# Conditioned residual stack (three adapter layers and paged attention): the first sequence's low parts moved from VectorE to GpSimd

## The chip, the cores and the metric

The kernel runs on 1 core of one Trainium2 chip. The metric is the time of one execution on the device in microseconds. Before the change it is 2490.15 us, the median of 3 runs (2487.76 to 2490.87).

## The reference

The input `x` is 64 sequences of 32 tokens with 512 features, float32. Four layers are added to it, one after the other:

```
x = x + x @ W0[adapter]^T                                 # per-sequence weight, 8 adapters
x = x + x @ W1^T + bias + scale * (x @ A1^T) @ B1^T       # LoRA of rank 16, 8 adapters
x = x + x @ W2^T + b + 2 * (x @ A2) @ B2                  # LoRA of rank 16, 32 slots
x = x + attention(x)
```

The attention projects to 32 query heads, 8 key heads and 8 value heads of 128. Queries and keys are divided by their root mean square, scaled and rotated by position. Each sequence attends to 512 cached keys, which a block table finds in 64 pages of 32 (masked beyond the sequence's length), and to its own 32 keys. Four query heads share one key head. Then comes the softmax, the product with the values and an output projection:

```
k_all = concat([k_cache[block_table], k], axis=1)
scores = where(valid, einsum('bqhd,bkhd->bhqk', q, k_all) / sqrt(128), -1e30)
o = einsum('bhqk,bkhd->bqhd', softmax(scores), v_all)
return einsum('bse,de->bsd', o, Wo)
```

## The kernel before

The kernel runs in stages on one core: `layer0` (to about 115 us), `lora_layers` (to about 290), `qkv` (the projections, to about 915), `attention` (to about 2390 with the start of the last stage inside it) and `output_projection`. Data between stages goes through DRAM.

Products whose precision matters are made in three passes (`three_pass`, lines 108 to 110). Each float32 operand is split into a high part, rounded by ScalarE to the matmul's own format (`fp32r`), and a low part, which is the operand minus its high part. The three products are high by high, high by low and low by high. The low parts are subtractions of two SBUF or PSUM operands.

**The projections.** `qkv` works through chunk pairs `b` of 32 steps `j`: 16 tiles of 128 tokens for each of two chunks of 512 columns (4 heads). The pair 0 makes the values, pairs 1 to 4 the queries, pair 5, the last, the keys. In every step after the values, TensorE multiplies tile `j` (12 matmuls of 512 columns) and turns the result of 4 steps before with four transposes (line 879). ScalarE takes the root of the sum of squares of the step before (`rms`, line 696), scales that step's product (`normed`, line 705, four instructions), squares the new product (line 690) and copies the turned tile of 4 steps before to `out_t` (line 715), which SyncE stores (line 640). VectorE's order in a step is: the first half of `part_b` of step j-2 (line 824), the reciprocal of step j-1 (`inv_rms`, line 808), `part_a` of step j-2 (line 817), the second half of `part_b` (line 824), their sum `rotated` (line 834), and the sum of squares of step j (line 812). `normed`, the tables `same` and `cross`, `part_a`, `part_b` and `rotated` all lie in SBUF. `normed` waits for the reciprocal, the reciprocal for the root, and the root for the sum of squares. In the steps 3, 6, 9 and 12 of a chunk a quarter of the next chunk's weights is split as well (lines 592 and 608). TensorE waits before a multiplication for the `normed` of four steps before (`normed_ready`), since the PSUM buffers turn round, and before a transpose for `rotated` and for the `out_t` copy of two steps before.

**What attention does ahead, in the last pair.** The first sequence's keys and queries are prepared while the last pair runs. There are six pieces: four of the cached keys (4 pages each, 128x1024), one of queries (128x1024, piece 3) and the sequence's own keys (128x256, piece 5). SyncE loads the pages in the steps of `PAGES_AHEAD`, GpSimd loads queries (`load_q`, line 1154) and own keys (`load_own_k`, line 1160). ScalarE makes the high part of a piece in the steps 13, 15, 17, 19, 21 and 25, at the end of its step (`scalar_ahead`, `hi_part`, line 1041, counted by `hi_done`). VectorE makes the low part one step later, at the end of its step (`vector_ahead`, `lo_part`, line 1051, counted by `lo_done`):

```
PIECES_AHEAD = {13: 0, 15: 1, 17: 2, 19: 3, 21: 4, 25: 5}
        if j - 1 in PIECES_AHEAD:
            lo_part(dve, 0, 0, PIECES_AHEAD[j - 1])
```

TensorE makes the scores of head 0 behind the last multiplication (step 31) and those of head 1 in the step behind that. Before head 0 it waits for all six low parts (`lo_done`). From then on the engines go over to attention. VectorE makes the low parts of all other sequences there, two steps of heads after the first scores at the earliest, and SyncE's page loads for later sequences wait for `lo_done` too.

**GpSimd's queue.** After the tables of the rotation (lines 673, 675 and 680, at 352 to 377 us) GpSimd has no work until the last pair. Its program in `attention` then is: wait for the stores of all queries, `load_q(0, 0)`; wait for the store of the keys of the first tile and for the row list; `load_own_k(0, 0)`; wait for the values' stores and the end of all projections (`mm_done`); a memset of the mask's columns, the loads of the second sequence's queries and own keys, a memset, and the value gathers of the first sequence.

**Attention.** For each of the 64 sequences and 8 key heads TensorE makes scores, transposes of the probabilities (line 1343) and the product with the values (line 1366). ScalarE makes the exponentials (line 1056), VectorE the mask and maximum (line 1080), and GpSimd the value gathers and the stores of the output.

Of the kernel before, what the change touches and what calls it, by code (L numbers as in the profile page):

```python
# [21 lines left out]
ALU = mybir.AluOpType  # L22
# [21 lines left out]
def f32(ap):  # L44

    return ap.bitcast(fp32)
# [66 lines left out]
def later(t, n):  # L113

    return not isinstance(t, int) or t >= n


def in_pairs(eng, n, body):

    body(0, False)  # L120
    with eng.Fori(1, n - 1) as i:
        body(i, False)
    body(n - 1, True)
# [354 lines left out]
ALL_STEPS = STEPS * (NB - 1)  # L478
# [455 lines left out]
PIECES_AHEAD = {13: 0, 15: 1, 17: 2, 19: 3, 21: 4, 25: 5}  # L934
# [15 lines left out]
def attention(nc, m, place, both, output, pool_sems, k_pages, v_pages, table, lens, key_at, q_t, k_own, v_own, o_t, inv_t):  # L950
# [34 lines left out]
    hi_done, lo_done, s_done, masked, pv_done = m.sem("hi_done"), both.lo_done, both.s_done, both.masked, both.pv_done  # L985
# [5 lines left out]
    def piece(c, p):  # L991

        if c == PIECE_Q:
            return q_raw[p][:, :], *(b[p][:, :, :].rearrange("p h q -> p (h q)") for b in (q_hi, q_lo))
        at, n = pages_of(c)
        return (k_raw[p][:, at:at + n, :].rearrange("p n (h k) -> p n h k", h=HK),
                *(b[p][:, :, at * PSIZE:(at + n) * PSIZE].rearrange("p h (n k) -> p n h k", n=n) for b in (k_hi, k_lo)))
# [33 lines left out]
    def raw_read(s, c):  # L1031

        return PIECES if not later(s, 3) else PIECES * (s - 2) + PIECE_TURN[c]
# [6 lines left out]
            act.wait_ge(s_done, HK * (s - 1))  # L1040
        act.activation(hi, raw, ACT.Copy).then_inc(hi_done, 1)  # L1041

    def lo_part(dve, s, p, c):

        raw, hi, lo = piece(c, p)
        turn = TURN_AHEAD[c] if not later(s, 1) else PIECES * s + PIECE_TURN[c]
        dve.wait_ge(hi_done, turn)
        if c == PIECE_Q and later(s, 1) and not later(s, 2):
            for n in range(2):
                dve.wait_ge(both.stored[n], 16 * ALL_STEPS // 2)  # L1050
        dve.tensor_tensor(lo, raw, f32(hi), ALU.subtract).then_inc(lo_done, 1)  # L1051

    def exponential(act, u, j):
        b = j % NB_P
# [16 lines left out]
    def make_mask(dve, s, p):  # L1071

        dve.tensor_scalar(mask[:, p, 0:NKEY], key_sb[:, :], lens_f[:, bass.ds(s, 1)], MASKED,
                          ALU.is_ge, ALU.mult).then_inc(lens_and_masks, 1)
        dve.wait_ge(lens_and_masks, s + 2)

    def mask_and_max(dve, u, j):

        b = j % NB_P
        dve.tensor_tensor_reduce(  # L1080
            out=prob[:, b, :].rearrange("p (a n) -> p a n", a=2), in0=ps_s[:, j % 2, :, 0:HALF],
            in1=mask[:, j // HK, :].rearrange("p (a n) -> p a n", a=2), scale=-SM_SCALE, scalar=3e38, op0=ALU.add, op1=ALU.min,
            accum_out=shift[:, b:b + 1]).then_inc(masked, 1)

    def vector_ahead(dve, j):

        if j == 4:
            dve.wait_ge(small_loaded, 48)
            dve.tensor_copy(lens_f[:, :], lens_sb[:, :]).then_inc(lens_and_masks, 1)
        if 4 <= j < 4 + PPP:  # L1090
            at = slice((j - 4) * PSIZE, (j - 3) * PSIZE)
            dve.tensor_copy(row_f[at, :], table_sb[at, :].rearrange("p (n m) -> p n m", m=PPP)[:, :, j - 4])\
               .then_inc(rows_ready, 1)
        if j == 4 + PPP:
            dve.wait_ge(rows_ready, PPP)
            dve.tensor_scalar(row_f, row_f, float(PSIZE), step_sb[:, 0:1], ALU.mult, ALU.add).then_inc(rows_ready, 1)
        if j == 5 + PPP:
            dve.wait_ge(rows_ready, PPP + 1)
            dve.tensor_copy(row_sb[:, :], row_f).then_inc(rows_ready, 1)
        if j - 1 in PIECES_AHEAD:  # L1100
            lo_part(dve, 0, 0, PIECES_AHEAD[j - 1])
        if j == STEPS:
            dve.wait_ge(lens_and_masks, 1)
            dve.wait_ge(zeroed, 2)
            make_mask(dve, 0, 0)
            dve.wait_ge(s_done, 1)
            mask_and_max(dve, 0, 0)
# [42 lines left out]
    def gpsimd(pool):  # L1150
        def load_q(s, p):
            if later(s, 2):
                pool.wait_ge(lo_done, raw_read(s, PIECE_Q))
            pool.dma_start(q_raw[p][:, :], q_t[bass.ds(s, 1)].rearrange("s d g x -> s d (g x)"))\
                .then_inc(k_loaded[p][PIECE_Q], 16)

        def load_own_k(s, p):
            if later(s, 2):
                pool.wait_ge(lo_done, raw_read(s, PIECE_OWN))
            pool.dma_start(k_raw[p][:, NPP, :], k_own[bass.ds(s, 1)]).then_inc(k_loaded[p][PIECE_OWN], 16)  # L1160

        def gather(s, p, c):

            pool.indirect_dma_start(  # L1164
                v_sb[p][:, c, :], None, v_pages.rearrange("n k x -> (n k) x"),
                bass.IndirectOffsetOnAxis(ap=rows_now[:, p, c:c + 1], axis=0)).then_inc(v_loaded[p], 16)

        def load_values(s, p):

            rows = v_own[bass.ds(s * SEQ, SEQ), :].rearrange("k (g u d) -> k g u d", g=HK // OG, u=OG)  # L1170
            for u in range(OG):
                if later(s, 2) and not u:
                    pool.wait_ge(pv_done, HK * (s - 1))
                if u == 1:
                    pool.tensor_copy(rows_now[:, p, :], row_sb[:, bass.ds(s * (NPP // PPP), NPP // PPP)])\
                        .then_inc(rows_copied, 1)
                    pool.wait_ge(rows_copied, s + 1)
                pool.dma_start(vo_sb[p][u * SEQ:(u + 1) * SEQ, :, u, :], rows[:, :, u, :])\  # L1178
                    .then_inc(own_v_loaded[p], 16)
                if u:  # L1180
                    gather(s, p, u - 1)

        def store_o(s, p):
            pool.wait_ge(o_ready, (HK // OG) * (s + 1))
            pool.dma_start(o_t[bass.ds(s, 1)], o_sb[:, p, :, :].rearrange("p h q -> p (h q)"))\
                .then_inc(o_stored[p], 16)

        def store_inv(s, p):
            pool.wait_ge(inv_ready, s + 1)
            pool.dma_start(inv_t[bass.ds(s, 1)].rearrange("s (h q) -> (s h) q", h=HK), inv_sb[:, p, :])\  # L1190
                .then_inc(inv_stored[p], 16)

        for p in range(2):
            pool.wait_ge(both.stored[p], 16 * (STEPS // 2) * (NB - 2))
        load_q(0, 0)
        pool.wait_ge(both.stored[0], 16 * ((STEPS // 2) * (NB - 2) + NT // 2 + 1))
        pool.wait_ge(rows_ready, PPP + 2)
        load_own_k(0, 0)
        for p in range(2):
            pool.wait_ge(both.v_stored[p], 16 * STEPS // 2)  # L1200
        pool.wait_ge(both.mm_done, ALL_STEPS)
        pool.memset(mask[:, :, NKEY:NALL], 0.0).then_inc(zeroed, 1)
        load_q(1, 1)
        load_own_k(1, 1)
        pool.memset(vo_sb[0][:, :, :, :], 0.0).then_inc(zeroed, 1)
        pool.wait_ge(zeroed, 3)
        load_values(0, 0)
        gather(0, 0, OG - 1)
        for p in range(2):
            pool.wait_ge(both.stored[p], 16 * ALL_STEPS // 2)  # L1210
        pool.memset(vo_sb[1][:, :, :, :], 0.0).then_inc(zeroed, 1)
        pool.wait_ge(zeroed, 4)

        def pair(i, last):


            for p in range(2):
                s = 2 * i + p
                if not last:
                    load_q(s + 2, p)  # L1220
                    load_own_k(s + 2, p)
                if not (last and p):
                    load_values(s + 1, 1 - p)
                if later(s, 1):
                    store_o(s - 1, 1 - p)
                if not (last and p):
                    gather(s + 1, 1 - p, OG - 1)
                if later(s, 1):
                    store_inv(s - 1, 1 - p)

        in_pairs(pool, NSEQ // 2, pair)
        store_o(NSEQ - 1, 1)
        store_inv(NSEQ - 1, 1)
# [102 lines left out]
    def tensor(pe):  # L1336
# [51 lines left out]
        in_pairs(pe, NSEQ // 2, pair)  # L1388

    return Ahead(sync_ahead, scalar_ahead, vector_ahead, tensor_ahead), Programs(sync, gpsimd, scalar, vector, tensor)  # L1390


# [727 lines left out]
```

## Time and profile before

| | before |
|---|---|
| median of 3 runs | 2490.15 us (2487.76 to 2490.87) |
| the profiled execution, its own time | 2487.61 us |
| its span | 2486.1 us |
| mean granted TensorE clock | 0.991 |
| TensorE matmul busy | 2414.1 us (97%) |
| VectorE busy | 1798.8 us (72%) |
| ScalarE busy | 1589.1 us (64%) |
| GpSimd busy | 696.5 us (28%) |
| HBM | 217 GB/s over the span |

All times of rows are microseconds from the start of the span of this one execution. Engines in the rows: PE is TensorE, PEld its weight load, DVE VectorE, ACT ScalarE, POOL GpSimd, SP SyncE. L12 is line 12 of the kernel. An instruction's recorded duration holds about 0.1 us of overlap with the next one on VectorE and ScalarE, so starts are compared with starts. The granted clock is a share of 2.4 GHz; 0.50 is the lower level, 1.2 GHz.

### The profile page before, as it was taken

How to read it: one execution, taken by the hardware profiler on the slowest of the kernel's cores; microseconds unless marked ns; L12 is line 12 of the kernel's file. 1: busy time of each engine (PE TensorE's matmuls, PEld its weight loads, DVE VectorE, ACT ScalarE, POOL GpSimd, SP SyncE). 2: the span in 40 equal slices, each digit the busy share in tenths (PEclk: the TensorE clock that was granted, in tenths of full speed). 3: DMA queues.
4: the chain of work that ended last, by engine and by line, in shares of the span. 5: the costliest groups of instructions: out<-in, count | busy, mean ns of one | idle time of the engine just before them, and what ended most of it. 6: DMA issues, size and time to landing. Idle time of an engine off the chain costs nothing.

```text
span 2486.1 us, 55755 instructions
## 1 busy us (share of the span) xinstructions
PE 2414.1 (97%) x16326; PEld 2196.7 (88%) x16327; DVE 1798.8 (72%) x3705; ACT 1589.1 (64%) x3325; POOL 696.5 (28%) x930
## 2 busy tenths in 40 slices
PE   6699999999999989999999999999999999999999
PEld 4588788888888779999999999999999999788887
DVE  6345445989998988888888887888888888644443
ACT  3122236777777778888888888888888888311111
POOL 1222130000000025455455445545445544000000
PEclk9899999999999999999999999999999999999999
DMA  7422442333333479888888888888888887766663
GB/s 240 140 76 76 147 140 89 101 102 112 102 98 102 128 211 313 294 290 295 304 285 293 302 290 287 289 305 285 297 300 283 295 300 269 271 228 213 211 210 138
DMA packets 377285, 541.48 MB, mean 218 GB/s; under 512 B 49522, under 2 KB 263218, under 8 KB 374386
## 3 DMA queue, kind: packets, MB, share of 16 engines
q1 hardware_dynamic: 305074, 316.33, 39.7%
q0 software_dynamic: 70016, 221.30, 25.8%
q10 hardware_dynamic: 2112, 2.89, 0.4%
q8 instruction: 34, 0.56, 0.1%
q14 instruction: 49, 0.40, 0.1%
HBM read 442.06 MB, written 98.30 MB: 217 GB/s over the span
## 4 chain that ended last, share of the span: by engine, by line
PE 62%; DMA 1%; DVE 1%; ACT 0%; issue 0%; DVEq 0%
PE both_ps_o L1366 18%; PE both_ps_s L108 10%; PE both_ps_s L110 10%; PE both_ps_s L109 10%; PE both_ps_pt L1343 9%; PE both_ps_o L1369 5%; DMA out_w<-in_wo 1%; PE both_ps_s L1349 1%; PE both_ps_s L1351 0%; DVE out_w_lo L1461 0%; ACT att_prob L1056 0%; DVE out_o_lo L1479 0%; DVE out_o L1475 0%; ACT out_w_hi L1457 0%; DVE att_prob L1080 0%
## 5 line engine op out<-in xcount | busy, mean ns | idle before, releaser
L1366 PE MATMUL both_ps_o<-att_pt,att_v 128*128 128x128 f32 x4096 | 539.3, 275 | 0.0
L1056 ACT ACTIVATE att_prob<-att_prob,att_shift 128x544 f32<-128x544 f32 x512 | 384.0, 750 | 204.7 <-DVE att_shift L1080 194.9
L1366 PEld LDWEIGHTS both_ps_o<-att_pt,att_v 128*128 128x128 f32 x4096 | 504.0, 191 | 0.0
L1080 DVE CUSTOM_DVE_ANT_0 att_prob<-both_ps_s,att_mask 128x544 f32<-128x544 f32 x512 | 365.9, 715 | 0.0
L1051 DVE TENSOR_TENSOR att_k_lo<-att_k_raw,att_k_hi 128x1024 fp32r<-128x1024 f32 (+1 forms) x320 | 338.2, 1057 | 1.9 <-ACT att_k_hi L1041 1.9
L108 PE MATMUL both_ps_s<-att_k_hi,att_q_hi 128*128 128x272 f32 x1024 | 338.3, 330 | 0.7 <-issue 0.6
L1164 POOL DMA_INDIRECT att_v<-in_v_pages,att_rows_now x256 | 299.6, 1170 | 85.0 <-issue 83.8
L1343 PE MATMUL both_ps_pt<-both_ident,att_prob 128*128 128x128 f32 x2048 | 308.2, 273 | 0.9 <-ACT att_pt L1240 0.9
L110 PE MATMUL both_ps_s<-att_k_hi,att_q_lo 128*128 128x272 f32 x1024 | 297.2, 290 | 0.0
L1240 ACT ACTIVATE att_pt<-both_ps_pt 128x512 f32<-128x512 f32 x512 | 294.8, 576 | 0.1
L109 PE MATMUL both_ps_s<-att_k_lo,att_q_hi 128*128 128x272 f32 x1024 | 294.4, 288 | 0.0
L1041 ACT ACTIVATE att_k_hi<-att_k_raw 128x1024 fp32r<-128x1024 f32 (+1 forms) x320 | 292.8, 915 | 0.0
L1178 POOL DMA_DIRECT2D att_vo<-v_own x256 | 144.4, 564 | 501.7 <-PE both_ps_o L1369 451.0
L1274 DVE COPY att_p_own<-att_prob 128x32 f32<-128x32 f32 x512 | 96.6, 189 | 221.9 <-PE both_ps_s L110 174.8
L1343 PEld LDWEIGHTS both_ps_pt<-both_ident,att_prob 128*128 128x128 f32 x2048 | 242.0, 142 | 1.3 <-ACT att_prob L1056 0.9
L1468 ACT ACTIVATE out_o_hi<-out_o 128x2048 fp32r<-128x2048 f32 x32 | 61.4, 1919 | 264.9 <-DVE out_o L1475 264.9
L108 PE MATMUL both_ps_s<-out_w_hi,out_o_hi 128*128 128x512 f32 x512 | 201.6, 394 | 5.5 <-DVE out_o_lo L1479 3.5
L110 PE MATMUL both_ps_s<-out_w_hi,out_o_lo 128*128 128x512 f32 x512 | 201.2, 393 | 0.0
L109 PE MATMUL both_ps_s<-out_w_lo,out_o_hi 128*128 128x512 f32 x512 | 201.2, 393 | 0.0
L1369 PE MATMUL both_ps_o<-att_pto,att_vo 128*128 128x128 f32 x1024 | 198.2, 275 | 0.0
L108 PEld LDWEIGHTS both_ps_s<-att_k_hi,att_q_hi 128*128 128x128 f32 x1024 | 194.3, 190 | 2.6 <-issue 1.1
L109 PEld LDWEIGHTS both_ps_s<-att_k_lo,att_q_hi 128*128 128x128 f32 x1024 | 195.2, 191 | 0.0
(195 smaller groups left out, 5153.1 us busy)
## 6 DMA issues: line engine op xcount, KB each, us to landing
att_k_raw<-in_k_pages SPq DMA_DIRECT2D x1024, 128.0 KB
q_t<-qkv_out_t SPq DMA_DIRECT2D x128, 256.0 KB, 2.3
att_q_raw<-q_t POOLq DMA_DIRECT2D x64, 512.0 KB
o_t<-att_o POOLq DMA_DIRECT2D x64, 512.0 KB, 6.7
out_o<-o_t SPq DMA_DIRECT2D x32, 1024.0 KB, 6.9
out_inv<-inv_t SPq DMA_DIRECT2D x32, 1024.0 KB, 6.9
qkv_w_stage<-in_w_qkv SPq DMA_DIRECT2D x12, 1024.0 KB, 5.2
early_stage<-in_w SPq DMA_DIRECT2D x10, 1024.0 KB, 7.0
```

Of the source, the lines that this page charges most:

```text
L108: pe.matmul(out, xh, wh, start=start, stop=False)
L109: pe.matmul(out, xh, wl, start=False, stop=False)
L110: return pe.matmul(out, xl, wh, start=False, stop=stop)
L1041: act.activation(hi, raw, ACT.Copy).then_inc(hi_done, 1)
L1051: dve.tensor_tensor(lo, raw, f32(hi), ALU.subtract).then_inc(lo_done, 1)
L1056: act.activation(prob[:, b, :], prob[:, b, :], ACT.Exp, bias=shift[:, b:b + 1], scale=-1.0, accum_out=total[:, j // HK, j % HK:j % HK + 1] ...
L1080: dve.tensor_tensor_reduce(out=prob[:, b, :].rearrange("p (a n) -> p a n", a=2), in0=ps_s[:, j % 2, :, 0:HALF], in1=mask[:, j // HK, :].re ...
L1164: pool.indirect_dma_start(v_sb[p][:, c, :], None, v_pages.rearrange("n k x -> (n k) x"), bass.IndirectOffsetOnAxis(ap=rows_now[:, p, c:c + ...
L1240: act.activation(pt_sb[:, j % OG, :, :], ps_pt[:, j % 2, :, :], ACT.Copy).then_inc(pt_ready, 1)
L1343: mm = pe.transpose(ps_pt[:, j % 2, c, :], prob[:, j % NB_P, c * P:(c + 1) * P], ident[:, :])
L1366: pe.matmul(out, v_sb[p][:, c, h * DH:(h + 1) * DH], pt_sb[:, j % OG, c, :], start=(c == 0), stop=False)
L1369: pe.matmul(out, vo_sb[p][:, g % 2, j % OG, :], pto_sb[:, g % 2, :], start=False, stop=True).then_inc(pv_done, 1)
```

## The change

`lo_part` is given the engine, and the six low parts of the first sequence are no longer issued in VectorE's last projection steps but in GpSimd's program. The first four (pieces 0, 1, 2, 3) stand behind `load_q(0, 0)`, each behind its wait for ScalarE's high part; the last two (pieces 4, 5) behind `load_own_k(0, 0)`. The instruction is the same subtraction and counts the same semaphore. All other sequences' low parts stay on VectorE.

```
-    def lo_part(dve, s, p, c):
+    def lo_part(eng, s, p, c):
 
         raw, hi, lo = piece(c, p)
         turn = TURN_AHEAD[c] if not later(s, 1) else PIECES * s + PIECE_TURN[c]
-        dve.wait_ge(hi_done, turn)
+        eng.wait_ge(hi_done, turn)
         if c == PIECE_Q and later(s, 1) and not later(s, 2):
             for n in range(2):
-                dve.wait_ge(both.stored[n], 16 * ALL_STEPS // 2)
-        dve.tensor_tensor(lo, raw, f32(hi), ALU.subtract).then_inc(lo_done, 1)
+                eng.wait_ge(both.stored[n], 16 * ALL_STEPS // 2)
+        eng.tensor_tensor(lo, raw, f32(hi), ALU.subtract).then_inc(lo_done, 1)
...
-        if j - 1 in PIECES_AHEAD:
-            lo_part(dve, 0, 0, PIECES_AHEAD[j - 1])
         if j == STEPS:
...
         load_q(0, 0)
+        first_pieces = list(PIECES_AHEAD.values())
+        for c in first_pieces[:4]:
+            lo_part(pool, 0, 0, c)
         pool.wait_ge(both.stored[0], 16 * ((STEPS // 2) * (NB - 2) + NT // 2 + 1))
         pool.wait_ge(rows_ready, PPP + 2)
         load_own_k(0, 0)
+        for c in first_pieces[4:]:
+            lo_part(pool, 0, 0, c)
         for p in range(2):
             pool.wait_ge(both.v_stored[p], 16 * STEPS // 2)
         pool.wait_ge(both.mm_done, ALL_STEPS)
```

## Rows read from the trace of the kernel before

**Rows 1.** What TensorE waited for, 846 to 915 us: us in total, times, longest.

```profile
PE both_ps_o L879 <- ACT qkv_out_t L715: 6.3, 7, 2.3
```

**Rows 2.** Chain that ended last, in order of time: start us, us, what.

```profile
912.78 0.70 DVE qkv_rotated L834
```

**Rows 3.** VectorE's groups, 846 to 903 us: count, busy us, mean ns, idle before.

```profile
L1051 DVE TENSOR_TENSOR att_k_lo<-att_k_raw,att_k_hi 128x1024 fp32r<-128x1024 f32 x4 | 4.9, 1214 | 0.0
```

**Rows 4.** ScalarE's timeline, one high part: start us, us, instruction, idle before.

```profile
861.68 1.09 ACT L1041 ACTIVATE att_k_hi<-att_k_raw 128x1024 fp32r<-128x1024 f32 x1
```

**Rows 5.** VectorE's timeline, one pair of steps with a piece.

```profile
862.99 0.18 DVE L808 RECIPROCAL qkv_inv_rms<-qkv_rms 128x4 f32<-128x4 f32 x1 [0.60 <-ACT qkv_rms L696]
863.09 0.66 DVE L817 TENSOR_TENSOR qkv_part_a<-qkv_normed,qkv_same 128x512 f32<-128x512 f32 x1
...
864.87 0.69 DVE L812 TENSOR_REDUCE qkv_sumsq<-qkv_squares 128x4 f32<-128x512 f32 x1
...
866.94 0.17 DVE L808 RECIPROCAL qkv_inv_rms<-qkv_rms 128x4 f32<-128x4 f32 x1
...
870.42 0.18 DVE L808 RECIPROCAL qkv_inv_rms<-qkv_rms 128x4 f32<-128x4 f32 x1 [0.60 <-ACT qkv_rms L696]
```

**Rows 6.** VectorE's timeline, plain steps and the step with the small low part.

```profile
887.66 0.18 DVE L808 RECIPROCAL qkv_inv_rms<-qkv_rms 128x4 f32<-128x4 f32 x1
...
890.59 0.18 DVE L808 RECIPROCAL qkv_inv_rms<-qkv_rms 128x4 f32<-128x4 f32 x1
...
893.07 0.42 DVE L1051 TENSOR_TENSOR att_k_lo<-att_k_raw,att_k_hi 128x256 fp32r<-128x256 f32 x1
...
893.74 0.17 DVE L808 RECIPROCAL qkv_inv_rms<-qkv_rms 128x4 f32<-128x4 f32 x1
```

**Rows 7.** GpSimd's table products and VectorE's weight subtractions, timeline, 354 to 379 us.

```profile
354.03 2.40 POOL L675 TENSOR_TENSOR qkv_cross<-qkv_sincos,qkv_norm 128x1024 f32<-128x1024 f32 x1
354.19 2.78 DVE L608 TENSOR_TENSOR qkv_w_lo<-qkv_w_stage,qkv_w_hi 128x512 fp32r<-128x512 f32 x1 [13.45 <-ACT qkv_w_hi L592]
...
361.56 2.40 POOL L673 TENSOR_TENSOR qkv_same<-qkv_sincos,qkv_norm 128x1024 f32<-128x1024 f32 x1
362.35 2.15 DVE L608 TENSOR_TENSOR qkv_w_lo<-qkv_w_stage,qkv_w_hi 128x512 fp32r<-128x512 f32 x1 [5.38 <-ACT qkv_w_hi L592]
...
378.67 0.69 DVE L608 TENSOR_TENSOR qkv_w_lo<-qkv_w_stage,qkv_w_hi 128x512 fp32r<-128x512 f32 x1 [6.62 <-ACT qkv_w_hi L592]
```

**Rows 8.** GpSimd's bias sums and a VectorE instruction beside them, timeline, 119 to 142 us.

```profile
119.81 3.61 POOL L1769 TENSOR_TENSOR lora_xb<-lora_x,early_stage 128x512 f32<-128x512 f32 x1 [2.54 <-DMA lora_x<-x]
...
131.17 2.51 POOL L1769 TENSOR_TENSOR lora_xb<-lora_x,early_stage 128x512 f32<-128x512 f32 x2 [7.75 <-DVE lora_x L1858]
131.39 0.69 DVE L1824 TENSOR_TENSOR lora_xt_lo<-both_ps_s,lora_xt_hi 128x512 fp32r<-128x512 f32 x1 [0.38 <-ACT lora_xt_hi L1786]
...
140.34 1.29 POOL L1769 TENSOR_TENSOR lora_xb<-lora_x,early_stage 128x512 f32<-128x512 f32 x1 [6.66 <-DVE lora_x L1858]
```

**Rows 9.** ScalarE's sines, GpSimd's start behind them and its slowest instructions, timeline.

```profile
349.50 2.01 ACT L736 ACTIVATE qkv_sincos<-qkv_wrapped 128x1024 f32<-128x1024 f32 x2
...
351.65 2.41 POOL L673 TENSOR_TENSOR qkv_same<-qkv_sincos,qkv_norm 128x1024 f32<-128x1024 f32 x1 [66.95 <-ACT qkv_sincos L736]
...
371.59 5.85 POOL L680 TENSOR_SCALAR qkv_cross<-qkv_cross 128x1024 f32<-128x1024 f32 x2
```

**Rows 10.** GpSimd's load of own keys, and TensorE's last turning transposes, timelines.

```profile
876.18 0.56 POOL L1160 DMA_DIRECT2D att_k_raw<-k_own  x1 [60.71 <-DMA k_own<-qkv_out_t]
...
900.26 0.60 PE L879 MATMUL both_ps_o<-both_ident,qkv_rotated 128*128 128x128 f32 x4
...
903.45 0.60 PE L879 MATMUL both_ps_o<-both_ident,qkv_rotated 128*128 128x128 f32 x4
```

**Rows 11.** TensorE behind a gap; then 1 us by engine (PE, PEld, DVE, ACT, POOL), clock, DMA.

```profile
43.02 0.66 PE L418 MATMUL l_ps_t<-l_ident,l_x 128*128 128x128 f32 x4 [1.64 <-DMA l_x<-in_x]
...
909.00:910.00 1.00, 0.00 (x0) 0.00 (x0) 0.91 (x3) 0.74 (x3) 1.00 (x1) 0.67 1.17 348
```

## The prediction

> **What bounds the kernel now.** I read the busy shares, then TensorE's waits, then the timelines of the last projection steps, and last the chain of waits over the hand-over to attention. TensorE is busy for 97% of the span, so VectorE time is worth something only where TensorE waits for it. Between 846 and 915 us it does: 6.3 us of waits at the turning transposes (line 879), for ScalarE's `out_t` copies [rows 1]. The chain enters attention through the last `rotated` [rows 2]. Between 858 and 915 us the pace is thus set by a loop of VectorE and ScalarE, and TensorE only follows. After it attention is paced by TensorE, so a shift of this hand-over reaches the end of the kernel whole.
>
> The loop per step: reciprocal (VectorE), `normed` and squares (ScalarE), sum of squares (VectorE), root (ScalarE), next reciprocal. A plain step takes 2.93 us from reciprocal to reciprocal [rows 6]. TensorE needs 3.19 us a step, as its turning transposes at 900.26 and 903.45 show [rows 10], so there the loop only catches up what it is behind. A pair of steps with one piece of the first sequence takes 7.43 us [rows 5]: 3.95 for the step that holds the low part, 3.48 for the one that holds the high part. TensorE's pair would be 6.4.
>
> **What the change removes.** Six low parts leave VectorE: five of 1024 columns at 1.21 us [rows 3] and one of 256 at 0.42 [rows 6]. A large one costs the loop 3.95 - 2.93 = 1.02 us. The small one costs 3.15 - 2.93 = 0.22. Removed from the loop: 5 x 1.02 + 0.22 = 5.32 us. With them gone a pair would take 6.41 us, as long as TensorE's, so most of the waits inside the projections would go too. If nothing came back, the hand-over would be 5.3 us earlier.
>
> **What it adds.** Six subtractions on GpSimd, each with two SBUF inputs. The nearest rows are GpSimd's 128x1024 products of lines 673 and 675 at 2.40 us [rows 7]. GpSimd is idle here, so its own time is free; its neighbours' is not. In the same rows two weight subtractions of VectorE, two SBUF inputs, normally 0.69 us, started while a GpSimd product ran and took 2.78 and 2.15. Taking off the usual length, they really began at 356.29 and 363.82 us, each 2.26 after the start of the GpSimd product. So such a product holds VectorE off for its whole length less 0.14. A VectorE instruction that reads one input from PSUM is not held: 0.69 us beside GpSimd [rows 8]. And when VectorE is already in a row of two-input instructions, GpSimd can be the one that waits: the first of its 128x512 sums took 3.61 us instead of 1.29 [rows 8].
>
> The Trainium skill says the same as a rule (SBUF — State Buffer, "SBUF: two separate sides"): the port pair shared by VectorE and GpSimd is an exclusive lock for a whole instruction, and a VectorE instruction with two SBUF inputs competes for it with a GpSimd one that reads SBUF. By this rule the change swaps a short occupation of VectorE for a longer blockade; the trace agrees, with 2.78 us against 0.69.
>
> Which VectorE instructions meet it? `part_a`, both halves of `part_b` and `rotated` have two SBUF inputs. The order in the loop decides. ScalarE's high part is followed by its root, and the reciprocal and `part_a` come right behind. Take the pair at 862 us: high part 861.68 + 1.09 = 862.77 [rows 4]. GpSimd starts 0.14 after a ScalarE result (349.50 + 2.01 = 351.51 to 351.65 [rows 9]), so at 862.91. `part_a` would start at 863.09 [rows 5], 0.18 later, and finds the port taken until 862.91 + 2.26 = 865.17: delayed by 2.08. From `part_a` on VectorE has no slack, since it reaches its sum of squares (1.88 us after the reciprocal) as soon as ScalarE has the squares; the next reciprocal is 2.08 later. Against 1.02 removed that is **+1.06 per large piece**, 5.3 for five. The small one: a line through 1.29 (512 columns) and 2.40 (1024) gives 0.74, 0.60 of it holding; GpSimd starts at 890.44 and holds until 891.04, `part_a` is due at 890.68 (a reciprocal at 890.59 [rows 6] and 0.09), so 0.36 against 0.22 removed, +0.14. **Sum +5.4 us.**
>
> Bounds of the unknown form (GpSimd writing the rounded low part over key strides): below, GpSimd comes too late for `part_a`, waits out VectorE's row of two-input instructions and starts with the sum of squares; then only what sticks out over that sum's 0.69 us [rows 5] delays, 2.26 - 0.69 = 1.57, +0.55 a piece, nothing for the small one (-0.22), +2.5 in all. Lowest of all, no blockade: -5.3. Above, each takes 2.93 us, half of the 5.85 of two, GpSimd's slowest instructions of this size [rows 9], +0.53 a piece, +8.1 in all. I take 2.40, the row with two inputs and the same size.
>
> **What moves with it.** TensorE is throttled by the loop from 858 us on, so its last projection, the page loads that wait for it, SyncE's stores, the mask memset and the value gathers all shift with the hand-over; SyncE's queue has no new wait. On GpSimd's queue the load of the first sequence's own keys is now behind the fourth low part. It is issued at 876.18 after waiting for a store [rows 10]; its high part, one pair behind the one at 861.68, ends at 870.2, and with 2.4 us the low part at 872.6, so the load keeps its time. The last low part then ends near 891 plus the shift of some 5 us, and the scores of the first head, which wait for all six, come behind the transposes at 903.45 [rows 10], with the same shift: 12 us of cover, so I cost this wait at nothing. Without the cover its price would be whatever the last piece is late. The memsets and gathers behind it wait for the end of the projections and are not passed. The high parts stay on ScalarE at their places. The executions before give 2487.61 for the profiled one (span 2486.1); with 5.4 that is 2493.0. The median of the runs, 2490.15, is 2.5 above it, so I predict **2495.6 us**. What a measurement of this kernel can tell from no change is 0.2%, 5.0 us; the forecast is just past it.
>
> **Rivals.**
> *No blockade.* GpSimd's subtraction runs beside `part_a` for free, 1.02 a piece comes back: 2490.15 - 5.3 = 2484.8, faster. For it: nothing but that the fp32r form is untried and that a fresh start may take the port later than 0.18 us after it is shown. Against it: both subtractions of [rows 7] were held. Chance 0.12, of which 0.08 past 0.2%.
> *GpSimd comes second.* VectorE's row of two-input instructions keeps the port, as in [rows 8]; +2.5, so 2492.7. The margin is 0.18 us, and it decides at zero. Chance 0.17, same.
> *TensorE's clock falls.* It now idles some 2.1 us per pair instead of 1.0. In the trace 1.64 us idle is followed by four transposes in 0.66 us, full clock, and at 909 us, after gaps of 1.5 and 2.3, the granted clock is down to 0.67 [rows 11]. At 1.2 GHz, the lower level, a step takes some 6 us against the loop's 4.2, so three steps at it lose 5 us more: 2500.8, slower. A gap of 2 us at one place in each pair decides. Chance 0.06.
> *First scores wait for GpSimd.* Needs a low part of over 12 us; in the 0.65 below.
>
> **How the numbers follow.** The forecast has 0.65. With the spread of the runs (2487.76 to 2490.87) and the uncertain length, three fifths of it are past 5.0 us: 0.39 slower, 0.26 same. With the rivals: slower 0.39 + 0.06 and 0.02 from longer instructions among the second rival's; same 0.26 + 0.15 + 0.04; faster 0.08. The range leaves out the first rival and part of the third: down to the second in a low run, 2487.76 + 2.5 = 2490.3, taken as 2490, up to the long bound in a high run, 2490.87 + 8.1 = 2499.
>
> **What would show it.** Right: `part_a` (line 817) of 2.7 us instead of 0.66 in five steps, reciprocals 5.0 and 3.5 us apart, more waits of TensorE at line 879, the last reciprocal 5 us later. Wrong: `part_a` at 0.66 throughout and a pair of 6.4 us (no blockade); GpSimd subtractions of 4 us and a late `part_b` (second rival); a granted clock under 1 between 858 and 900 us (third).

## The result and the profile after

The changed kernel takes 2495.47 us in the median of 17 runs (2490.22 to 2499.38), the kernel before 2490.15 in the median of 17 (2486.55 to 2493.44). The ratio is 1.002 with a 95% interval of 1.0013 to 1.0026: slower, by 5.0 us (3.2 to 6.5). Whether it is past the 5.0 us that the prediction set as its threshold stays open.

| | before | after |
|---|---|---|
| the profiled execution, its own time | 2487.61 us | 2497.33 us |
| its span | 2486.1 us | 2495.8 us |
| mean granted TensorE clock | 0.991 | 0.991 |
| VectorE busy | 1798.8 us | 1804.4 us |
| GpSimd busy | 696.5 us | 712.0 us |
| TensorE matmul busy | 2414.1 us | 2414.2 us |

VectorE lost six instructions and is 5.6 us busier. Where that comes from is seen in the timelines of the last projection steps. Here is the second piece after the change, out of the timelines of VectorE, ScalarE and GpSimd. [rows 4, 5] show the third piece before; the five large pieces are alike. The columns are start us, us, instruction, idle time before it; "..." stands for further lines of the timeline.

```profile
858.79 1.10 ACT L1041 ACTIVATE att_k_hi<-att_k_raw 128x1024 fp32r<-128x1024 f32 x1
...
859.96 2.40 POOL L1051 TENSOR_TENSOR att_k_lo<-att_k_raw,att_k_hi 128x1024 fp32r<-128x1024 f32 x1 [5.98 <-ACT att_k_hi L1041]
860.10 0.18 DVE L808 RECIPROCAL qkv_inv_rms<-qkv_rms 128x4 f32<-128x4 f32 x1 [0.60 <-ACT qkv_rms L696]
860.19 2.71 DVE L817 TENSOR_TENSOR qkv_part_a<-qkv_normed,qkv_same 128x512 f32<-128x512 f32 x1
...
863.94 0.68 DVE L812 TENSOR_REDUCE qkv_sumsq<-qkv_squares 128x4 f32<-128x512 f32 x1
...
864.98 0.18 DVE L808 RECIPROCAL qkv_inv_rms<-qkv_rms 128x4 f32<-128x4 f32 x1
```

GpSimd starts 0.07 us behind the end of the high part (858.79 + 1.10 = 859.89). `part_a` is issued 0.23 later and lasts 2.71 instead of 0.66: it really began at 862.24, 2.28 after GpSimd. The step that follows, with the next high part, still takes 3.49 us from reciprocal to reciprocal (to 868.47), the one in which GpSimd subtracts 4.88 instead of 3.95. The pair takes 8.37 instead of 7.43. All five large pieces look like this (`part_a` 2.72, 2.71, 2.72, 2.72 and 2.72 us). The small one takes GpSimd 0.78 us from 898.69 on, and `part_a` beside it 1.02.

TensorE's waits for `rotated` between 846 and 924 us (in total, times, longest):

```profile
PE both_ps_o L879 <- DVE qkv_rotated L834: 7.1, 5, 1.6
```

All five lie in the steps with pieces (855 to 890 us). Before, TensorE waited there four times for `out_t`, 0.55 us each, 2.2 us in total. The rest of the 6.3 us in [rows 1], 4.1 us, lies behind 904 us, at the hand-over to attention; so [rows 1] says less about the steps with pieces than the prediction took from it. After the change the `out_t` waits at the hand-over come to 6.2 us. TensorE's idle time rose in the steps with pieces, but its clock stayed at full speed. One window of the changed kernel, columns: length, busy of PE, PEld, DVE, ACT and POOL with counts, granted clock, DMA share, GB/s:

```profile
858.00:880.00 22.00, 17.99 (x85) 13.39 (x84) 19.79 (x30) 15.50 (x40) 7.20 (x3) 1.00 0.22 60
```

From 880 to 900 us the granted clock is 1.00 as well.

The span differs by 9.7 us, more than the runs do. The reciprocals split it (a reciprocal is named by the step in which VectorE issues it). In step 3, before the change touches anything, the profiled execution after is 3.3 us later (812.60 against 809.28); that is the scatter of the stages before. From there to step 14 it loses 0.3, over the 18 steps from the reciprocal of step 14 to the last one 4.74 (65.00 against 60.26 us), over the hand-over, up to TensorE's first transpose of attention's own probabilities (924.48 us before, 933.40 after), 0.6, and 0.8 in the 1560 us behind. The 4.74 are the change; whether the 0.6 belong to it is taken up behind the rivals.

From here on this stretch of 18 steps serves as the measure of the loop. Each kernel's was profiled once, but in all eight profiles the steps that no subtraction touches last 2.91 to 2.94 us, or 3.48 to 3.50 with a high part, while whole executions scatter by several us.

### The profile page after: what moved, and what is told of

It reads as the page before. It is cut to its first block, busy times and chain, and to the rows that moved or that the text cites. A ratio compares the mean times of both kernels' runs of the same rounds, so it can differ in the third digit from the quotient of the medians.

```text
span 2495.8 us, 55755 instructions
## 1 busy us (share of the span) xinstructions
PE 2414.2 (97%) x16326; PEld 2196.3 (88%) x16327; DVE 1804.4 (72%) x3699; ACT 1587.9 (64%) x3325; POOL 712.0 (29%) x936
## 4 chain that ended last, share of the span: by engine, by line
PE 61%; DMA 1%; ACT 1%; DVE 1%; issue 0%; ACTq 0%; DVEq 0%
PE both_ps_o L1369 18%; PE both_ps_s L108 10%; PE both_ps_s L110 10%; PE both_ps_s L109 9%; PE both_ps_pt L1346 9%; PE both_ps_o L1372 5%; DMA out_w<-in_wo 1%; PE both_ps_s L1352 1%; PE both_ps_s L1354 0%; DMA k_own<-qkv_out_t 0%; ACT att_prob L1056 0%; ACT att_k_hi L1041 0%; DVE out_w_lo L1464 0%; DVE out_o_lo L1482 0%; DVE out_o L1478 0%
## 5 line engine op out<-in xcount | busy, mean ns | idle before, releaser
L1051 DVE TENSOR_TENSOR att_k_lo<-att_k_raw,att_k_hi 128x1024 fp32r<-128x1024 f32 x315 | 333.2, 1058 | 1.9 <-ACT att_k_hi L1041 1.9
L1162 POOL DMA_INDIRECT att_v<-in_v_pages,att_rows_now x256 | 305.0, 1191 | 85.0 <-issue 83.8
```

Of the source, the lines that this page charges most:

```text
L1051: eng.tensor_tensor(lo, raw, f32(hi), ALU.subtract).then_inc(lo_done, 1)
L1162: pool.indirect_dma_start(v_sb[p][:, c, :], None, v_pages.rearrange("n k x -> (n k) x"), bass.IndirectOffsetOnAxis(ap=rows_now[:, p, c:c + ...
```

## The experiments

The theory was: GpSimd's subtractions hold VectorE's two-input instructions for their length, this sets the loop back, and the loop's shift reaches the end whole. Four kernels tested its parts against the rivals; two more asked whether GpSimd can be used without the hold.

**A fill instead of the subtraction.** GpSimd writes zeros. Its queue, waits and order stay; the low parts of the first sequence are left out of the computation.

```
+        if not later(s, 1):
+            eng.memset(f32(lo), 0.0).then_inc(lo_done, 1)
+            return
         eng.tensor_tensor(lo, raw, f32(hi), ALU.subtract).then_inc(lo_done, 1)
```

> GpSimd fills the first sequence's six low parts with zeros instead of subtracting (they are left out of the computation; waits, order and semaphores as in the changed kernel). Theory (a blockade by GpSimd instructions that read SBUF, and its shift reaches the end whole): part_a 0.66 us in every step, reciprocals 2.93 and 3.48 us apart in a pair, the last reciprocal 5 us earlier than in the kernel before, time 5.3 us under it (ratio 0.998). Rival A (any GpSimd instruction holds VectorE): a fill of 1.0 us delays part_a by some 0.65 us, pair 7.1 us, ratio 0.9993. Rival B (the changed kernel is slower for GpSimd's queue or the later own-key load, not for the blockade): the time stays at that of the changed kernel, ratio 1.002.

Measured: 2484.96 us against 2489.93 before, ratio 0.9979 (0.9970 to 0.9988). Timelines of GpSimd and VectorE:

```profile
863.10 0.95 POOL L1052 MEMSET att_k_lo<- 128x1024 f32 x1 [5.45 <-ACT att_k_hi L1041]
863.26 0.18 DVE L808 RECIPROCAL qkv_inv_rms<-qkv_rms 128x4 f32<-128x4 f32 x1 [0.60 <-ACT qkv_rms L696]
863.36 0.66 DVE L817 TENSOR_TENSOR qkv_part_a<-qkv_normed,qkv_same 128x512 f32<-128x512 f32 x1
...
869.67 0.18 DVE L808 RECIPROCAL qkv_inv_rms<-qkv_rms 128x4 f32<-128x4 f32 x1 [0.60 <-ACT qkv_rms L696]
```

`part_a` starts 0.26 us into a 0.95 us fill and takes its usual 0.66. The pair takes 6.41 us, the 18 steps 54.89, 5.37 less than before. Both rivals fall: an instruction that only writes does not hold VectorE, and the order in GpSimd's queue, with the load of the own keys behind four pieces, costs nothing. It also gives the price of six low parts on VectorE, 5.4 us of loop, and shows that this arrives at the end.

**A copy instead of the subtraction**, with one SBUF input; the subtraction of the first sequence's high parts is left out.

```
+        if not later(s, 1):
+            eng.tensor_copy(lo, raw).then_inc(lo_done, 1)
+            return
         eng.tensor_tensor(lo, raw, f32(hi), ALU.subtract).then_inc(lo_done, 1)
```

> GpSimd copies the raw piece into the low part (one SBUF input instead of two; the low parts of the first sequence are wrong values, the subtraction is left out). Theory (every GpSimd instruction that reads SBUF takes the shared port for its length): part_a in the five steps grows by the copy's duration less 0.14 less the 0.2 us of its head start; if the copy takes 1.2 us, part_a is 1.5 us. Rival (only two-input GpSimd instructions hold): part_a stays 0.66 us and the pair takes 6.4 us.

```profile
862.26 1.04 POOL L1052 CAST att_k_lo<-att_k_raw 128x1024 fp32r<-128x1024 f32 x1 [5.96 <-ACT att_k_hi L1041]
...
862.51 1.33 DVE L817 TENSOR_TENSOR qkv_part_a<-qkv_normed,qkv_same 128x512 f32<-128x512 f32 x1
```

`part_a` is held for 0.67 us: it began at 863.18, 0.92 after GpSimd. The copy takes 1.04, so it too holds for its length less 0.12, as the theory had it. Reading one operand is enough. The step costs the loop 0.59 us (3.52 against 2.93), the 18 steps take 57.89. One execution, 2486.27 us, too few to compare the time.

**The subtraction moved behind the squares**, so that it meets the sum of squares first; `j` is the step of the piece's high part.

```
+        def late(c):
+            j = [j for j, piece_at in PIECES_AHEAD.items() if piece_at == c][0]
+            pool.wait_ge(both.squared, STEPS * (NB - 2) + j + 2)
+            lo_part(pool, 0, 0, c)
+
         for c in first_pieces[:4]:
-            lo_part(pool, 0, 0, c)
+            late(c)
...
```

> Each GpSimd subtraction waits also for ScalarE's squares of the next step, so that it starts with VectorE's sum of squares instead of with part_a. Theory (the hold counts only where VectorE has a two-input instruction due; the sum of squares has one input and runs beside it): part_a back to 0.66 us, the first half of part_b delayed by 1.6 to 1.7 us, next reciprocal 1.6 us late instead of 2.0, time 2.5 us over the kernel before (ratio 1.001). Rival (VectorE is held whatever its instruction reads): the sum of squares itself takes 2.7 us and the time is that of the changed kernel, ratio 1.002.

```profile
866.93 0.69 DVE L812 TENSOR_REDUCE qkv_sumsq<-qkv_squares 128x4 f32<-128x512 f32 x1
866.98 2.38 POOL L1051 TENSOR_TENSOR att_k_lo<-att_k_raw,att_k_hi 128x1024 fp32r<-128x1024 f32 x1 [5.61 <-ACT qkv_squares L690]
867.53 2.10 DVE L824 TENSOR_TENSOR qkv_part_b<-qkv_normed,qkv_cross 128x256 f32<-128x256 f32 x1
```

The sum of squares (one input) takes its 0.69 us beside GpSimd. The first half of `part_b` behind it is held 1.68 us, and the step takes 4.51 to 4.54. The 18 steps take 62.91 us, 2.65 over before, 2.09 under the change. Time: 2491.67 against 2489.93, ratio 1.0006 (0.9997 to 1.0015), so not shown to be slower than before by the time alone, and its interval just overlaps the changed kernel's (1.0013 to 1.0026). The difference between these kernels rests on the loop. The same subtraction on the same engine costs the loop 1.6 us instead of 2.0 when it starts some 2 us later in the step.

**VectorE, but in its idle time**: the kernel before, with four low parts at the head of the steps 16, 18, 20 and 22.

```
+LO_FIRST = {16: 0, 18: 1, 20: 2, 22: 3}
...
+                if is_last(b) and j in LO_FIRST:
+                    ahead.vector_first(dve, j)
                 if is_step(b, j, 2):
                     cross_part(*step_before(b, j, 2), 0)
...
-        if j - 1 in PIECES_AHEAD:
+        if j - 1 in PIECES_AHEAD and PIECES_AHEAD[j - 1] not in LO_FIRST.values():
             lo_part(dve, 0, 0, PIECES_AHEAD[j - 1])
...
+    def vector_first(dve, j):
+        lo_part(dve, 0, 0, LO_FIRST[j])
```

> The kernel before, with the low parts of pieces 0 to 3 still on VectorE but at the head of the steps 16, 18, 20 and 22, where VectorE sits idle 0.6 to 0.7 us for ScalarE's root behind the next high part. Theory (the loop is what counts, and idle VectorE time inside it is free): each such low part costs the loop 0.45 instead of 1.02 us, together 2.2 us, ratio 0.9991. Rival (VectorE's total work sets the pace, not its place): no change against the kernel before, ratio 1.000.

```profile
862.70 0.18 DVE L808 RECIPROCAL qkv_inv_rms<-qkv_rms 128x4 f32<-128x4 f32 x1
...
865.18 1.21 DVE L1053 TENSOR_TENSOR att_k_lo<-att_k_raw,att_k_hi 128x1024 fp32r<-128x1024 f32 x1
...
866.65 0.17 DVE L808 RECIPROCAL qkv_inv_rms<-qkv_rms 128x4 f32<-128x4 f32 x1
...
869.57 0.18 DVE L808 RECIPROCAL qkv_inv_rms<-qkv_rms 128x4 f32<-128x4 f32 x1
```

The steps take 3.95 and 2.92 instead of 3.95 and 3.48: a low part now shares a step with the next piece's high part, and the 0.60 us for which VectorE waited are filled. The 18 steps take 57.90 us (-2.36), so the place in the loop counts and not VectorE's total work. Ratio 0.9991 (0.9982 to 1.0000), 2488.38 us against 2489.93; the size is the expected one, and the interval just reaches no change, so by the time alone the gain is not shown.

**Small slices at the right moment.** Pieces 0, 1, 2 and 4 on GpSimd in four slices of 256 columns, one per step, each released by that step's squares; piece 3 in VectorE's idle time of step 22; the small piece on VectorE as before.

```
+        for n in range(16):
+            pool.wait_ge(both.squared, STEPS * (NB - 2) + 14 + n + 1)
+            lo_slice(pool, LO_POOL[n // 4], n % 4)
+            if n == 8:
+                pool.wait_ge(both.stored[0], 16 * ((STEPS // 2) * (NB - 2) + NT // 2 + 1))
+                pool.wait_ge(rows_ready, PPP + 2)
+                load_own_k(0, 0)
```

> The low parts of pieces 0, 1, 2 and 4 on GpSimd in four slices of 256 columns each, one slice per step 14 to 29, each started by ScalarE's squares of that step, so that it runs beside VectorE's sum of squares (one input, 0.6 us); piece 3 on VectorE in the idle time of step 22, the own keys on VectorE as in the kernel before; the load of own keys behind the ninth slice. Theory (a hold costs only what sticks out over one-input VectorE time): a slice holds the port 0.60 to 0.64 us from 0.14 us behind the squares, sticks out 0.15, costs the loop 0 to 0.1 a step. The 18 steps from the first high part to the last reciprocal take 54.9 + 0.5 + 0.2 + (0 to 1.6) = 55.6 to 57.2 us against 60.3 in the kernel before; ratio 0.9981 to 0.9988. Rival (every crossing of a GpSimd subtraction costs VectorE its whole length wherever it is put): 16 x 0.64 = 10 us on top of 55.6, slower than the kernel before, ratio 1.002.

```profile
856.40 0.69 DVE L812 TENSOR_REDUCE qkv_sumsq<-qkv_squares 128x4 f32<-128x512 f32 x1
856.45 0.74 POOL L1071 TENSOR_TENSOR att_k_lo<-att_k_raw,att_k_hi 128x256 fp32r<-128x256 f32 x1 [2.18 <-ACT qkv_squares L690]
857.01 0.46 DVE L824 TENSOR_TENSOR qkv_part_b<-qkv_normed,qkv_cross 128x256 f32<-128x256 f32 x1
```

A slice starts 0.05 us into the sum of squares, and the next two-input instruction is held by 0.04 us, less than the loop's slack there. The steps take 2.93 and 3.49, as with the fill. The 18 steps take 55.74 us (-4.52), within the expected 55.6 to 57.2. That is 0.85 more than with the fill: 0.52 in the step with piece 3, 0.27 in the one with the small piece, so the sixteen slices cost less than 0.1 us together. Between 846 and 900 us TensorE no longer waits, with these slices as with the fill. Its last transposes at the hand-over still do, 5.1 and 4.7 us, so there the loop still sets the pace.

Time: 2484.17 us against 2489.75, ratio 0.9978 (0.9969 to 0.9988). The ratio lies just under the expected 0.9981 to 0.9988, well within the interval. This version computes everything and is faster than the kernel before, and so than the changed one.

**The same slices without timing**, four in a row behind each high part in the changed kernel.

```
-            lo_part(pool, 0, 0, c)
+            for i in range(4):
+                lo_slice(pool, c, i)
```

> The changed kernel with each large subtraction on GpSimd cut into four of 256 columns, issued one behind the other without a timing of their own. Theory (the port is held per instruction; VectorE gets in between two of them): part_a is held for the rest of the first slice only, 1.1 us instead of 2.7, and the later slices take longer than their 0.78 us because they wait for VectorE's two-input instructions; the rest comes back as a held first half of part_b, pair between 7.5 and 8.4 us. Rival (GpSimd keeps the port over instructions in a row): part_a 3.0 us or more, pair 8.7 us or more.

```profile
848.77 3.91 POOL L1068 TENSOR_TENSOR att_k_lo<-att_k_raw,att_k_hi 128x256 fp32r<-128x256 f32 x4 [32.32 <-ACT att_k_hi L1042]
...
848.98 1.06 DVE L817 TENSOR_TENSOR qkv_part_a<-qkv_normed,qkv_same 128x512 f32<-128x512 f32 x1
849.97 0.96 DVE L824 TENSOR_TENSOR qkv_part_b<-qkv_normed,qkv_cross 128x256 f32<-128x256 f32 x1
851.01 1.06 DVE L834 TENSOR_TENSOR qkv_rotated<-qkv_part_a,qkv_part_b 128x512 f32<-128x512 f32 x1
852.00 0.67 DVE L812 TENSOR_REDUCE qkv_sumsq<-qkv_squares 128x4 f32<-128x512 f32 x1
```

`part_a` is 1.06 us, as expected, and a pair (4.13 + 3.49 = 7.62) is in the expected range. But the rest does not come back at the first half of `part_b`, where I put it. The engines take turns: each of the three two-input instructions is held by 0.4 to 0.5 us, and GpSimd's four slices, 0.74 each when alone, take 3.91 us together. The last slice ends at 852.68, with the sum of squares, so nothing is left for the first half of `part_b` behind it (0.41 us). The 18 steps take 61.21 us, between before and the change; one execution, 2489.85 us.

**Loop and time together.** "Loop" is the 18 steps, one profiled execution each; the time is the ratio minus one, of 2490 us.

| kernel | loop, us | against before | time against before |
|---|---|---|---|
| before | 60.26 | | |
| changed | 65.00 | +4.74 | +5.0 (3.2 to 6.5) |
| fill, nothing subtracted | 54.89 | -5.37 | -5.2 (-7.5 to -3.0) |
| subtraction behind the squares | 62.91 | +2.65 | +1.5 (-0.7 to +3.7) |
| VectorE's idle time | 57.90 | -2.36 | -2.2 (-4.5 to 0.0) |
| timed slices | 55.74 | -4.52 | -5.5 (-7.7 to -3.0) |

Every loop difference lies within the interval of its time. Each interval is some 2 us wide to either side and would by itself allow a part of the shift to be lost; taken together, a straight line through nought fitted to the five gives 1.02 us of time per us of loop. So the shift reaches the end whole as far as these runs can tell, in both directions.

## Why the prediction was right

*What bounds the kernel.* The loop of VectorE and ScalarE set the hand-over, and its shift reached the end, as the table shows.

*What the change removes.* 5.32 us by the intervals of plain steps against steps with a low part; the fill gives 5.37. "A pair would take 6.41 us" was measured as 6.41.

*What it adds.* The hold was sized from two rows of another stage [rows 7] at 2.26 us behind GpSimd's start; it was 2.28 here, and `part_a` 2.7 us long, as said. (By those rows as printed, with 0.69 us taken off, it is 2.25, which changes nothing.) The step costs 4.88 to 4.90 us, so the change adds 0.93 to 0.95 per large piece, not 1.06. So the size of this term was too high. Two small things make it up. GpSimd started 0.07 us behind the high part, not 0.14 as behind the sines [rows 9]. And the stretch from the real start of `part_a` to the sum of squares is 1.70 us when VectorE works without waits (862.24 to 863.94), 1.78 in [rows 5]: a slack of some 0.1 that I had taken for none. The small piece added 0.04 (3.19 against 3.15), not 0.14. The sum is +4.7 for the loop against +5.4. The median came out 5.3 above that of before, and the ratio says 5.0; that the forecast of 2495.6 met 2495.47 so closely is luck within a scatter of several us between runs (2490.22 to 2499.38), with a loop term 0.7 too large.

*What moves with it.* The own keys were loaded at 881.80 us and not at 876.18, still on waiting for their store and not for the low part, which had ended at 879.11; the last low part ended at 899.5, 12 us before TensorE's transposes behind the last multiplication at 911.83. The place in GpSimd's queue cost nothing, which the fill also shows.

*The rivals.* "No blockade" is out: five of five large subtractions held `part_a`. The Trainium skill's rule (SBUF — State Buffer, "SBUF: two separate sides") holds in this kernel in three points: a two-input VectorE instruction is held by a GpSimd instruction that reads (2.71 us, and 1.33 with the copy), not by one that only writes (0.66), and a one-input VectorE instruction is not held (0.69). "GpSimd comes second" did not happen, but the experiment that forced it gave +2.65 for the +2.5 of its working. TensorE's clock stayed at 1.00 from 846 to 900 us with one wait of up to 1.6 us per pair, where the prediction had put 2.1. At the hand-over the clock falls to the lower level with or without the change: for 10.2 us from 909.3 on before, for 6.8 us from 919.2 on after. Before, it fell inside the gap of 2.3 us and not behind it, as the prediction reads [rows 11]. The shorter stretch belongs to the slower kernel, so the clock does not explain the slow-down.

One thing at the hand-over was not in the prediction: in the changed kernel's profile ScalarE waits 1.68 us for an `out_t` store to land, 0.41 before. The chain of that profile enters attention through this store (6.44 us from 913.21 on). The stretch from the last reciprocal to the first transpose of own probabilities is 16.7 us there, 16.1 before, and 16.1 to 16.4 in the six experiments. The wait is not the changed kernel's alone: with the subtraction behind the squares it is 1.39 us (stretch 16.4), in the other five at most 0.52. These are the two kernels with the longest loop, so 0.6 us or less of the 5.0 may come from the store; one profile each cannot tell it from scatter, and no run tests it.

## What to carry to other kernels

In this kernel, moving work from VectorE to an idle GpSimd relieves VectorE only if its neighbours in time do not need two SBUF inputs: while a GpSimd instruction that reads SBUF runs, they wait for all but the last 0.12 to 0.15 us of it, and a two-input GpSimd instruction takes twice as long as VectorE's own (2.40 us against 1.21). Look at which instruction is due when GpSimd starts; small GpSimd instructions that begin together with a one-input VectorE instruction of about the same length (0.74 and 0.69 us) cost next to nothing. And before moving work away, look for the idle time that the loop leaves on the busy engine itself: it gave 2.36 of the loop's possible 5.37 us by a change of order alone.

## What the runs showed of the hardware that I had not expected

- With four slices in a row, GpSimd and VectorE took turns: slices of 0.74 us and two-input instructions alternated one by one. In [rows 8] they did not: that sum took 3.61 us instead of 1.29, so it began at 122.13 us, when a row of five VectorE subtractions (four from 119.20 on, one from 121.61) was ending. Both readings stand; no run shows what decides between them.
- The hold is shorter than GpSimd's recorded duration by nearly the same amount whatever the length: 0.12 us for subtractions of 2.40 and 0.78 us and a copy of 1.04 us, 0.14 or 0.15 for the slices of 0.74 us and for the subtractions behind the squares. So it can be read off the duration.
- A GpSimd copy of 128x1024 takes 1.04 us, less than VectorE's subtraction (1.21), while GpSimd's own multiplication by a constant took 2.93 [rows 9] and its two-input instructions 2.40. The number of inputs alone does not order them.
